# An attention and expert layer on one core: value products in two halves of the queries, ring items one by one, statistics four tiles at a time

## The reference

```
x = x + LN(attention(LN(x)))   # attention: z + proj(softmax(q k^T / 4) v), 16 heads of width 16,
                               # q, k, v from a weighted layer norm of z, all in f32
x = x + LN(ffn(LN(x)))         # ffn: a shared gated layer of 128 hidden units for all tokens;
                               # 512 routed tokens are also sent to one of 8 experts
```

## Time and profile before

| | us |
|---|---|
| median of 3 runs | 983.62 (983.3 to 984.05) |
| the profiled execution | 983.9 |
| its span | 982.1 |
| TensorE busy | 882.3 (90%) |
| VectorE busy | 792.7 (81%) |
| ScalarE busy | 663.7 (68%) |
| GpSimd busy | 314.5 (32%) |
| mean granted TensorE clock | 0.968 of 2.4 GHz |

### The profile page before, as it was taken

How to read it: one execution, slowest core, us unless ns; L and a number is a source line. 1 busy time by engine, 2 the same in 40 slices (tenths; PEclk the granted TensorE clock), 3 DMA queues, 4 the chain that set the end, 5 groups by cost and what they waited for, 6 DMA issues and landing times. The chain is left out here.

```text
span 982.1 us, 14337 instructions
## 1 busy us (share of the span) xinstructions
PE 882.3 (90%) x5188; PEld 319.8 (33%) x5188; DVE 792.7 (81%) x1568; ACT 663.7 (68%) x728; POOL 314.5 (32%) x450
## 2 busy tenths in 40 slices
PE   6879999999999999999999999999989989757985
PEld 3312322222243233322332242322322313136863
DVE  4598879898979878899888879889799788265765
ACT  5128778787877787878877868788677768901110
POOL 4041010005424414139443423255243232822113
PEclk9769999999999999999999999999999989988998
DMA  5631010310320203101411022004310001240001
GB/s 143 105 45 39 16 53 16 73 41 10 90 61 13 93 12 70 38 13 55 89 61 56 12 39 59 23 7 105 91 56 14 11 13 31 85 172 23 1 1 64
DMA packets 52375, 49.08 MB, mean 50 GB/s; under 512 B 17504, under 2 KB 43696, under 8 KB 51920
## 3 DMA queue, kind: packets, MB, share of 16 engines
q1 hardware_dynamic: 51680, 46.91, 19.4%
q0 software_dynamic: 384, 1.05, 0.3%
q10 hardware_dynamic: 240, 0.20, 0.2%
HBM read 18.06 MB, written 9.17 MB: 28 GB/s over the span
## 5 line engine op out<-in xcount | busy, mean ns | idle before, releaser
L1331 DVE TENSOR_REDUCE mx<-ring 128x1 f32<-128x512 f32 x1024 | 633.9, 680 | 110.3 <-PE ring L1038 109.6
L873 ACT ACTIVATE prob<-sc,unscale 128x1024 f32<-128x1024 f32 x512 | 539.1, 1113 | 85.2 <-PE sc L1056 83.9
L1038 PE MATMUL ring<-kp,qp 48*128 48x512 f16 x1024 | 299.4, 395 | 43.5 <-DVE mx L1331 22.5
L1070 PE MATMUL obank<-prob,vaug 128*32 128x512 f32 x2048 | 276.1, 612 | 0.7 <-ACT prob L873 0.6
L1038 PEld LDWEIGHTS ring<-kp,qp 48*128 48x128 f16 x1024 | 74.1, 93 | 361.4 <-DVE mx L1331 301.3
L1056 PE MATMUL sc<-qp,kp 64*128 64x512 f16 x1024 | 167.9, 381 | 14.0 <-ACT prob L873 13.3
L644 POOL TENSOR_TENSOR parts<-qkf,parts 128x1024 f16<-128x1024 f32 x14 | 29.9, 2134 | 209.6 <-ACT parts L803 209.6
L1056 PEld LDWEIGHTS sc<-qp,kp 64*128 64x128 f16 x1024 | 50.4, 95 | 92.3 <-ACT prob L873 83.9
L631 POOL TENSOR_TENSOR hid<-hid,b 128x512 f32<-128x512 f32 x24 | 30.2, 1270 | 110.9 <-ACT hid L827 110.9
L639 POOL TENSOR_TENSOR yA<-yA,sums 128x512 f32<-128x512 f32 x15 | 19.0, 1269 | 131.1 <-DMA sums<-reciprocal_scratch 131.1
L1070 PEld LDWEIGHTS obank<-prob,vaug 128*32 128x32 f32 x2048 | 40.5, 108 | 61.5 <-issue 58.4
(11 more groups left out here) (221 smaller groups left out, 749.2 us busy)
## 6 DMA issues: line engine op xcount, KB each, us to landing
x_sb<-x SPq DMA_DIRECT2D x7, 1024.0 KB, 6.0
kp<-parts SPq DMA_DIRECT2D x48, 128.0 KB, 4.4
qp<-parts SPq DMA_DIRECT2D x93, 64.0 KB, 5.5
out<-hid SPq DMA_DIRECT2D x4, 1024.0 KB, 5.3
yA<-oT SPq DMA_DIRECT2D x124, 32.0 KB
sums<-reciprocal_scratch SPq DMA_DIRECT2D x31, 128.0 KB
x_scratch<-x SPq DMA_DIRECT2D x3, 1024.0 KB, 4.5
qp<-mp SPq DMA_DIRECT2D x128, 2.0 KB
```

Source lines behind the costliest of these rows:

```text
L873: nc.scalar.activation(prob[:, e % 2, 2 * a:2 * a + 2, :].rearrange("p g n -> p (g n)"), sbuf2[a][:, :], ACT.Exp, scale=unscale[:, 0:1]).t ...
L1038: nc.tensor.matmul(dst[:, :], qp[rows, qh, h, qt * P:(qt + 1) * P], kp[rows, h, kh * HALF:(kh + 1) * HALF], start=True, stop=True).then_in ...
L1070: ins = nc.tensor.matmul(obank[i * VW:(i + 1) * VW, :], vaug[:, b % 2, kt, c0:c0 + VW], prob[:, v % 2, i, :], start=(kt == 0), stop=(kt == ...
L1331: nc.vector.tensor_reduce(mx[:, u % 2, n:n + 1], src[:, :], AX.X, ALU.max).then_inc(rv_free, 1)
```

## The change

The value product of a slot is cut into two halves of 256 queries. The order on TensorE in a slot becomes: items, max products 0 and 1, `scores(0)`, value half 0 of `e - 1`, max products 2 and 3, `scores(1)`, value half 1 of `e - 1`. The waits of the value product (for both exponentials of its slot, for the copy of `obank`) stand ahead of half 0. Items that stood two in a slot are spread to one in a slot. Of VectorE's statistics, `Y_STATS` (2 tiles each) moves to four slots, those of `u` are cut in two times 4 tiles, in slots 51 and 53 (`U_STATS`), and `Z_STATS`, `F_AT` go from both in one slot to one in each of two. The two gates move from slots 47 and 49 to 50 and 53, the two tanh of ScalarE from 46 and 48 to 48 and 51, and GpSimd's chains behind `y`, `u` and one `second_part` by two to four slots.

```diff
-QK_AT = (2, 2, 4, 4)
-Z_AT = ((18, 18, 20, 20), (9, 9, 17, 17))
-V_AT = (25, 25, 49, 49)
-P_AT = (19, 19, 21, 21)
-QK_NEXT_AT = (33, 33, 35, 35)
-X_AT = (41, 41, 42, 42)
-H_AT = (44, 44, 47, 47)
-U_AT = (57, 57)
-W_AT = (59, 59, 61, 61)
+QK_AT = (1, 2, 4, 5)
+Z_AT = ((17, 19, 21, 23), (9, 11, 13, 15))
+V_AT = (26, 28, 51, 53)
+P_AT = (17, 19, 22, 24)
+QK_NEXT_AT = (33, 35, 37, 39)
+X_AT = (41, 42, 43, 44)
+H_AT = (45, 46, 48, 49)
+U_AT = (57, 58)
+W_AT = (59, 60, 61, 62)
...
-Z_STATS = ((9, 10), (2, 2))
-Y_STATS = (21, 21, 25, 25)
+Z_STATS = ((9, 10), (1, 2))
+Y_STATS = (19, 22, 24, 26)
 X_STATS = (33, 35)
-F_AT = ((4, 4), (0, 1))
...
-D_AT = (43, 51, 14, 19)
+U_STATS = (51, 53)
+F_AT = ((4, 5), (0, 1))
...
+D_AT = (43, 51, 14, 20)
...
-                if 1 <= w < B and tau == 25:
+                if 1 <= w < B and tau == 27:
                     mean_of("y", w - 1, 0, D)
...
-                if w + 1 < B and tau == 34:
+                if w + 1 < B and tau == 36:
                     second_part(w + 1, 0)
...
-                if 1 <= w < B and tau == 50:
+                if 1 <= w < B and tau == 54:
                     mean_of("u", w - 1, 0, F)
...
-                if 1 <= w < B and tau in (46, 48):
-                    i = int(tau == 48)
+                if 1 <= w < B and tau in (48, 51):
+                    i = int(tau == 51)
                     sc.wait_ge(s_added["h"], 4 * (w - 1) + 2 * i + 2)
                     tanh(2 * (w - 1) + i, 4 * i, 4)
...
-                def value_product(v):
+                def value_product(v, half):
+
+                    cols = slice(half * HALF // 2, (half + 1) * HALF // 2)
                     u, kt = v // 8, v % 8
                     b, g = u // HU, u % HU // NH
-                    if kt == 0 and u > 0:
+                    if kt == 0 and u > 0 and half == 0:
                         pe.wait_ge(s_oT, u)
...
-                    pe.wait_ge(s_free, 2 * v + 2)
+                    if half == 0:
+                        pe.wait_ge(s_free, 2 * v + 2)
                     for i in range(GH):
                         c0 = (g * GH + i) * VS
-                        ins = nc.tensor.matmul(obank[i * VW:(i + 1) * VW, :], vaug[:, b % 2, kt, c0:c0 + VW],
-                                               prob[:, v % 2, i, :], start=(kt == 0), stop=(kt == NT - 1))
-                    ins.then_inc(s_av, 1)
+                        ins = nc.tensor.matmul(obank[i * VW:(i + 1) * VW, cols], vaug[:, b % 2, kt, c0:c0 + VW],
+                                               prob[:, v % 2, i, cols], start=(kt == 0 and half == 0),
+                                               stop=(kt == NT - 1), skip_group_check=True)
+                    if half == 1:
+                        ins.then_inc(s_av, 1)
...
                 if 0 <= e < NS:
                     scores(0)
-                    scores(1)
+                if 0 <= e - 1 < NS:
+                    value_product(e - 1, 0)
...
                 if t < NS:
                     max_products(range(2, 4))
+                if 0 <= e < NS:
+                    scores(1)
                 if 0 <= e - 1 < NS:
-                    value_product(e - 1)
+                    value_product(e - 1, 1)
...
-                if 1 <= w < B and tau in (47, 49):
-                    n = int(tau == 49)
+                if 1 <= w < B and tau in (50, 53):
+                    n = int(tau == 53)
```

More of the change, by code:

```diff
@@ L1058, in scores @@
                     ins.then_inc(s_full, 1)
-                def value_product(v):
+                def value_product(v, half):
+                    cols = slice(half * HALF // 2, (half + 1) * HALF // 2)
                     u, kt = v // 8, v % 8
                     b, g = u // HU, u % HU // NH
-                    if kt == 0 and u > 0:
+                    if kt == 0 and u > 0 and half == 0:
                         pe.wait_ge(s_oT, u)
-                    if v % SL == 0:
+                    if v % SL == 0 and half == 0:
                         pe.wait_ge(ra_free, TAKEN["v", b, 3][1] + 1)
-                    pe.wait_ge(s_free, 2 * v + 2)
+                    if half == 0:
+                        pe.wait_ge(s_free, 2 * v + 2)
                     for i in range(GH):
                         c0 = (g * GH + i) * VS
-                        ins = nc.tensor.matmul(obank[i * VW:(i + 1) * VW, :], vaug[:, b % 2, kt, c0:c0 + VW],
-                                               prob[:, v % 2, i, :], start=(kt == 0), stop=(kt == NT - 1))
-                    ins.then_inc(s_av, 1)
+                        ins = nc.tensor.matmul(obank[i * VW:(i + 1) * VW, cols], vaug[:, b % 2, kt, c0:c0 + VW],
[3 more added lines that the diff above has]
+                        ins.then_inc(s_av, 1)
                 def items():
@@ L1440, in _ @@
                     nc.vector.tensor_tensor(half, half, sums[0:GH * HD, 1, :], ALU.mult).then_inc(s_div64, 1)
-                if 1 <= w < B and tau in (47, 49):
-                    n = int(tau == 49)
+                if 1 <= w < B and tau in (50, 53):
+                    n = int(tau == 53)
                     gate_first(2 * (w - 1) + n, act[:, 4 * n:4 * n + 4, :], hid[:, 4 * n:4 * n + 4, 0:F])
                     gate_second(2 * (w - 1) + n, act[:, 4 * n:4 * n + 4, :], hid[:, 4 * n:4 * n + 4, F:2 * F])
-                if 1 <= w < B and tau == 49:
-                    ve.wait_ge(s_mean["x"], w)
-                    for i in range(2):
+                if 1 <= w < B:
+                    for i in slots_of(tau, U_STATS):
+                        if i == 0:
+                            ve.wait_ge(s_mean["x"], w)
                         ve.wait_ge(s_hc, 4 * (w - 1) + 2 * i + 2)
                         ins = stats_of("u", act, 4 * i, 4, F)
-                    ins.then_inc(s_stats["u"], 1)
+                        if i == 1:
+                            ins.then_inc(s_stats["u"], 1)
                 for key in RING_AT[t]:
```

## The result

| | before | after |
|---|---|---|
| median | 983.71 (983.3 to 986.9, 11 runs) | 987.35 (986.32 to 990.32, 11 runs) |
| the profiled execution | 983.9 | 987.4 |
| its span | 982.1 | 985.6 |

The direction was right, the size was not.

What follows compares the result with a forecast made beforehand. The prediction took waits between engines, a loop in each slot, to bound the kernel, not one busy engine. Gains of 9.8, 4.8 and 0.8 us against costs of 7.4, 7.2, 4.7, 1.7, 1.0 and 2.5 gave 983.6 + 9.1 = 992.7, range 977 to 1003.

Steps and rivals of the forecast that it cites:

- The plain slot: Slot without an item: 2.49 to 2.45 us through a new ScalarE loop; -0.04 in 244 slots, -9.8 us.
- `scores(1)` to the start of its exponential 0.49: Piece of ScalarE's new loop through value half 0: 0.49 us of the loop's 2.45.
- `nm` and `mt`: Slots with `mt` and `nm`: some 0.75 us when alone, 0.3 more beside one transpose; sum +4.7 us.
- `qk`: Two ScalarE steps per `qk` item make value half 0 late: 0.5 us each for 18 items, net +7.4 us.
- the rival in which VectorE becomes the limit: Plain slots at 2.39, terms of `qk`, `obank` and tail gone: 967 us; chance 0.17 together with a half near 0.52.
- `obank`: Value half 0 waits for the copy of `obank`: 0.5 us in 12 slots, 0.4 at three with a transpose, +7.2.
- the tail: Twelve slots behind the last max product: 2.22 us each instead of 2.01, +2.5 us.
- One f32 item in a slot: TensorE is the limit: slot 4.15 to 4.2 us, item 1.75 instead of 1.83; 60 items, -4.8 us.
- The gate of slot 50: VectorE's gate in a middle batch's slot without an item shows 1.27 us; with slot 53's 0.45, +3.4 over two batches.
- The last batch: Gates and statistics there: slots 49 and 50 fall from 5.5 to 4.3 us, `Y_STATS` saves 1.4; -2.4 us.
- Even: Rival: late terms (`qk`, `obank`, `mt`) meet existing waits and half of their 19 us goes: 983 us; chance 0.13.
- Slower by far: Rival: gates in plain slots stop TensorE and its clock falls, 6 x 1.3 = 8 us: 1001 us; chance 0.12.

Runs made afterwards that it cites:

- Experiment 4: Changed kernel with a second, already fulfilled wait (on `s_av`) ahead of ScalarE's exponential 1; 992.19 us, ratio 1.0071 to the kernel before.
- experiment 8: Changed kernel with VectorE's first gate in slot 51 instead of 50; 987.27 us, ratio 1.0042 to the kernel before.
- experiment 1: New TensorE order with value halves, but all slot numbers, gates and statistics of the kernel before; 985.78 us, ratio 1.0005 to the kernel before.
- experiment 6: New order, old slot numbers, old order behind `obank` copies, `qk` items and the last max product, in and behind transpose slots; 978.21 us, ratio 0.9934 to before.
- experiment 7: Changed kernel with the old order behind the `obank` copy, behind `qk` items and behind the last max product; 981.33 us, ratio 0.9968 to the kernel before.
- experiment 3: Kernel before with the value product cut in two adjacent halves at its old place; 985.41 us, ratio 1.0007 to the kernel before.

## Why the prediction was right or wrong

**The plain slot: the step that failed.** It is "`scores(1)` to the start of its exponential 0.49", as the prediction put it. The two rows behind it show `scores(0)` and exponential 0, and exponential 0 has a wait instruction more than exponential 1 (on `s_av`, so that `prob` may be written again). It measured 0.42. ScalarE's loop is then 0.05 + 0.57 + 0.23 + 0.42 + 1.11 = 2.38, not 2.45, and with VectorE's 2.39 beside it the plain slot is 2.39. Experiment 4 put the instruction there and got 2.45. Plain slots at 2.39 were the prediction's own sign of being wrong. The mechanism, a new loop through ScalarE, was right, and a term of it was mis-sized by 0.06.

A second step was wrong with it: the loop was taken to set all 142 slots without an item, so that 0.06 would be 8.5 us. Experiment 4 moves 59 slots. Behind an item TensorE is busy all of 2.28 (490.12:492.40), and the slots with `nm` and `mt` and those around a `qk` item are as long with the second wait as without it.

The prediction saw the first doubt ("its wait for `scores(1)` is in no row") and gave it to the rival in which VectorE becomes the limit. That rival's condition came true, but its price did not: it let the terms of `qk`, `obank` and the tail go as well. They stayed, since a ScalarE step of 0.6 is ten times the room that 0.06 makes.

**The sum, set right.** Experiment 4 is the changed kernel with the mis-sized term made as large as forecast. It is 7.5 us slower than before by the medians, the changed kernel is 3.6 slower, and +9.1 was forecast. So the step is worth some 4 (3.9 by the medians, 4.1 by the traces) of the 5.5 by which the forecast was too high, and some 1.5 lie in the other terms. What the traces show of these:
- The slots behind the last max product cost 1.5 in all, not 2.5: where nothing else stands they take 2.17 instead of 2.22 (2.23 in experiment 4), and three of the twelve did not grow.
- `nm` and `mt` alone take 5.51 over two slots, where the sum has 2 x 2.45 + 0.75 = 5.65. Behind items one behind the other a slot takes 2.28, where the sum has 2.45.
- Against that, 17 slots from slot 14 on in which VectorE joins the maxima (`nm`) stay at 2.47 to 2.50, where the sum has 2.45.
- Also against it, slots 33 and 34 of the last batch took 4.86 + 2.87 in the profiled execution; experiment 8, the same there, took 3.99 + 2.39. The difference, 1.35, is the clock's (below).

This is no full account, slot by slot; that it came as near as this is in part luck, since errors of both signs met.

**Terms that measured as forecast.** A half: 0.57. One f32 item in a slot: 4.21 and 4.20 where two such slots follow each other (forecast 4.20); where a plain slot follows, 4.31 + 2.28, the same as 4.20 + 2.39. A `w` item: 3.34. A `qk` item: 4.83 instead of 4.31, so +0.52 (0.5). The copy: +0.48 (0.5). `nm` with `mt` alone: 2.81 + 2.69 over two slots of 2.39, +0.72 (0.75, but over slots of 2.45). The gate of slot 50: 5.65 - 4.31 = 1.34 (1.27); the one of slot 53 with its statistics 2.69 - 2.28 = 0.41 (0.45). One transpose: 2.98 and then 2.29, together 5.27 (forecast 0.36 + 4.90 = 5.26).

**The last batch** was put at -2.4 for gates and statistics. Slots 40 to 55 gave 2.45, of which some 0.2 for each of its four `h` items belongs to the item term; what is left is 1.6, in slots whose clock no longer falls. The other gains of that batch, 2.5, came in slots 16 to 31. Nearly half of them is the clock again: slot 26 of before took 3.66 at a granted clock of 0.53, and 2.50 at 1.00 in experiment 1, where the items and statistics stand as before. The forecast had 1.4 there, all of it for the statistics that moved beside the `p` items.

**The other rivals.** "Even", in which the late terms meet waits that are there anyway, did not happen: the copy, the `qk` items and `mt` each showed. That the time, 987.35, lies between that rival's 983 and the forecast is chance. "Slower by far" did not either. The gate in slot 50 makes TensorE wait, but the granted clock stays 1.00 there (592.47:598.12). The mechanism itself is at work elsewhere, in the last batch of experiments 4, 6, 7 and 8.

**Layout changes.** The rows of before had 0.10 for going into the layout of the value product, and the halves kept to it: 0.32 from 526.52 to 526.84, against 0.22 for a couple. Coming out of it once more costs 0.13 (experiment 3). Together 0.23, forecast 0.24. The Trainium skill, TensorEngine Tiling (Array Packing), Instruction Overhead, gives each matmul some 60 cycles; experiment 3, with eight records more in every slot, has none of it in its plain slots (2.49).

## What to carry to other kernels

When a loop is added up from starts, take each piece from the very instruction that stands in the loop: its neighbour on the same line of code may have one wait more, and 0.06 us a slot made some 4 of the 5.5 us of this error. Then ask in which slots that loop is the limit, for it was so in far fewer than were counted. A product cut in two to free the engine ahead of it pays only where the engine behind has nothing extra to do; here the old order in one slot of eight, behind the copy, turned +1.1 us into -5.7. Look for that slot before spreading work evenly. And take a set of moves apart: the slot numbers as a whole cost 4.7, 1.2 and 2.1 us a batch under the old, the new and the mixed order, but without the two gates some 3.2, nothing and 0.5. What spreading items costs depends on the order around them, and the gate that lost its cover cost 1.2 to 1.3 under each.

## What the runs showed that was not expected

**A fulfilled wait has a price**: 0.06 us ahead of one ScalarE instruction (0.42 to 0.48), and some 4 us for the kernel, where it lies in the loop that sets 59 of the slots.

**Twice the matmul records cost almost nothing**: 16 of 256 columns in 1.01 us, 8 of 512 in 1.00.

**The clock can fall behind the same wait in one kernel and not in another.** In slot 33 of the last batch TensorE waits 0.91 for VectorE, in the changed kernel and in experiment 8 alike. In the changed kernel the granted clock then fell to 0.51, the lower level of 1.2 GHz, and was back at 1.00 by 742.77:

```profile
736.16:739.04 2.88, 1.88 (x14) 0.45 (x14) 2.85 (x9) 1.55 (x2) 0.00 (x0) 1.00 0.00 1
739.04:741.02 1.98, 1.98 (x12) 0.33 (x13) 1.74 (x3) 0.91 (x1) 0.00 (x0) 0.51 0.04 7
741.02:742.77 1.75, 1.75 (x16) 0.33 (x12) 1.11 (x2) 0.82 (x2) 0.00 (x0) 0.58 0.21 63
```

In experiment 8 it stayed at 1.00:

```profile
734.04:738.03 3.99, 2.99 (x25) 0.72 (x25) 3.96 (x11) 2.02 (x3) 0.00 (x0) 1.00 0.02 4
738.03:740.42 2.39, 2.38 (x28) 0.64 (x25) 2.39 (x6) 2.23 (x3) 0.00 (x0) 1.00 0.17 54
```

What decides between them these runs don't tell. Experiments 6 (1.4 us in the same slots) and 7 (slots 53 and 54 at 5.91 + 3.96, clock 0.75 and 0.51) lost to it as well, so a difference of one or two microseconds between such kernels may be the clock's and not the change's.
